# Second layer's A and B operands split ahead of the first step, in a two-layer FFN kernel on one core

## The reference, cut to what matters

```
# layer 0: mixing of channels by weights that depend on the condition, then a base product with LoRA
agg_w = einsum('bk,koi->boi', softmax(mlp(cond)), weight)    # a 32x32 matrix for each batch
c0    = einsum('boi,bih->boh', agg_w, x) + agg_b
x     = x + c0 @ W_base.T + b_base + sum over 4 experts of alpha_e * 2 * (c0 @ A_e.T) @ B_e.T
# layer 1: a grouped convolution of 9 taps along the columns, then a base product with LoRA, top 2 of 28
c1     = conv(x, weight, groups=4) + cond @ c_weight.T + bias
logits = c1 @ gate_W.T                                       # the two largest, with a softmax
x      = x + c1 @ base_W.T + (gate * 2 * (c1 @ lora_A.T)) @ lora_B.T
```

## Time and profile before

| what | value |
|---|---|
| median of 3 runs | 385.61 us (385.39 to 385.76) |
| the profiled execution, own time | 385.73 us |
| its span | 383.8 us |
| PE, DVE, ACT, POOL busy | 97%, 70%, 32%, 15% of the span |
| granted TensorE clock | 0.998 of full speed |

### The profile page before, as it was taken

The page is one execution under the profiler, slowest core; times in us unless marked ns, Lnnn a source line. Parts: engine busy times, 40 slices in busy tenths (PEclk is TensorE's granted clock), DMA queues, the critical chain, the costliest instruction groups (busy, mean ns, idle before and its releaser), DMA issues.

```text
span 383.8 us, 9759 instructions
## 1 busy us (share of the span) xinstructions
PE 373.9 (97%) x3199; PEld 328.6 (86%) x3199; DVE 270.4 (70%) x935; ACT 122.6 (32%) x380; POOL 56.9 (15%) x180
## 2 busy tenths in 40 slices
PE   8999899999999999999999999999999999998996
PEld 8899689888888988888899888889988888887684
DVE  5679887676667767766786676668767666776754
ACT  6656333323323332231233323223332322222211
POOL 5459700000000000000000000000000000010000
PEclk9999999999999999999999999999999999999999
DMA  7765677655566775555767655576765556566631
GB/s 230 257 201 141 166 192 194 186 130 154 160 170 170 186 186 132 163 155 159 185 170 192 151 147 154 154 188 164 192 170 141 151 154 154 140 172 160 160 87 55
DMA packets 71018, 63.05 MB, mean 164 GB/s; under 512 B 4030, under 2 KB 53502, under 8 KB 70872
## 3 DMA queue, kind: packets, MB, share of 16 engines
q1 hardware_dynamic: 70998, 62.82, 61.5%
q10 hardware_dynamic: 2, 0.00, 0.0%
HBM read 45.75 MB, written 16.91 MB: 163 GB/s over the span
## 4 chain that ended last, share of the span: by engine, by line
PE 85%; DVE 4%; DMA 4%; SPq 3%; issue 2%; ACT 1%; ACTq 0%; DVEq 0%
PE p_chy L980 14%; PE p_chy L986 14%; PE p_chy L981 14%; PE p_u L980 8%; PE p_u L986 8%; PE p_chy L1124 8%; PE p_u L981 8%; PE p_t L1136 3%; PE p_y L980 2%; PE p_y L981 2%; PE p_y L986 2%; DMA b_raw<-b_raw 2%; DMA win<-x_scratch 1%; PE p_y L1108 1%; PE p_y L1109 1%
## 5 line engine op out<-in xcount | busy, mean ns | idle before, releaser
L980 PE MATMUL p_u<-w_hi,xt_hi 128*128 128x256 f32 (+1 forms) x256 | 69.2, 297 | 0.7 <-DVE w_lo L727 0.3
L981 PE MATMUL p_u<-w_lo,xt_hi 128*128 128x256 f32 (+1 forms) x256 | 67.1, 288 | 0.0
L821 DVE STREAM_TRANSPOSE c<-p_chy 128x512 f32<-128x512 f32 x32 | 22.9, 716 | 54.1 <-PE p_chy L1124 54.1
L539 ACT CAST u_hi<-p_u 128x256 fp32r<-128x256 f32 x64 | 24.9, 389 | 100.3 <-PE p_u L986 100.3
L591 ACT CAST g1t_hi<-p_t 112x256 fp32r<-112x256 f32 x32 | 12.0, 374 | 121.0 <-PE p_t L1136 121.0
L980 PE MATMUL p_chy<-w_hi,c_hi 128*128 128x512 f32 x124 | 49.7, 401 | 0.3 <-DVE w_lo L747 0.3
L980 PEld LDWEIGHTS p_u<-w_hi,xt_hi 128*128 128x128 f32 x256 | 48.1, 188 | 1.6 <-issue 0.7
L981 PE MATMUL p_chy<-w_lo,c_hi 128*128 128x512 f32 x124 | 48.6, 392 | 0.0
L981 PEld LDWEIGHTS p_u<-w_lo,xt_hi 128*128 128x128 f32 x256 | 48.2, 188 | 0.0
L986 PE MATMUL p_u<-w_hi,xt_lo 128*128 128x256 f32 (+1 forms) x256 | 42.9, 290 | 0.0
L986 PEld LDWEIGHTS p_u<-w_hi,xt_lo 128*128 128x128 f32 x256 | 36.2, 189 | 0.0
(11 more groups left out here) (164 smaller groups left out, 788.0 us busy)
## 6 DMA issues: line engine op xcount, KB each, us to landing
win<-x_scratch SPq DMA_DIRECT2D x96, 256.0 KB, 4.0
x_scratch<-x SPq DMA_DIRECT2D x32, 260.0 KB, 2.1
xt_sb<-in_xt SPq DMA_DIRECT2D x32, 256.0 KB, 4.9
x_sb<-in_x SPq DMA_DIRECT2D x32, 256.0 KB, 4.8
out<-y_sb SPq DMA_DIRECT2D x32, 256.0 KB, 4.0
w_sb<-in_w SPq DMA_DIRECT2D x4, 256.0 KB, 5.3
w_sb<-in_w SPq DMA_DIRECT2D x1, 1024.0 KB, 5.3
a_sb<-in_a SPq DMA_DIRECT2D x1, 504.0 KB, 7.6
```

What stands on the lines that cost most here:

```text
L539: nc.scalar.copy(u_hi[:, t.mod(4), cols], p_u[:, banks]).then_inc(u_hi_done[half], 1)
L821: V.transpose(c1[:], p_cv).then_inc(c1_tr, 1)
L980: mm(psum, lhs_hi, rhs_hi, start=start and n == 0, stop=False)
L981: mm(psum, lhs_hi, rhs_lo, start=False, stop=False)
```

## The change

Everything named here is computed as before; the order and the engines of some one-time work differ.

- a1 is loaded by ACT's queue, behind the second gelu. b1 takes its slot in SP's queue, behind w1.
- Ahead of the first step ACT writes a_hi, copies p_mix to mix_raw (both halves) and writes b_hi before u_hi of tile 1, half b. DVE writes a_lo and, in one piece, b_lo, which POOL did in four.
- w1's split moves up: the two w_hi into steps 0 and 1, both w_lo into step 1.
- ACT's constant rows of the windows' slot 1 move to the third step, behind xt_hi; PE waits for them before the second convolution instead of the first.
- b_round and mix_hi of tile 1 on ACT move behind the first exponent of layer 0's gates, into the first step.
- POOL's late mix copies are put into a function, with the same order and place.

```diff
             sp.dma_start(w_sb[:], w1.rearrange("p (c d) -> p c d", c=HC)).then_inc(ld_w1, 16)
-            sp.dma_start(a1_sb[:], a1.rearrange("p (c n) -> p c n", c=HC)).then_inc(ld_a1, 16)
+            sp.dma_start(b1_sb[:], b1.rearrange("p (a d) -> p a d", a=2)).then_inc(ld_b1, 16)
...
-            b1_v = b1.rearrange("p (a d) -> p a d", a=2)
-            sp.dma_start(b1_sb[:], b1_v).then_inc(ld_b1, 16)
...
+            def late_mix(blocks):
+
+                for k in blocks:
+                    pool.tensor_copy(*raw_blocks(k // BT, k % BT)).then_inc(mix_rest_done, 1)
+                    pool.wait_ge(mix_rest_done, k + 1)
+
...
-                        for n in range(BT):
-                            for b in range(BT):
-                                pool.tensor_copy(*raw_blocks(n, b)).then_inc(mix_rest_done, 1)
-                                pool.wait_ge(mix_rest_done, n * BT + b + 1)
+                        late_mix(range(0, MIX_REST))
...
-                if at(s, 1):
-                    pool.wait_ge(b1_hi_done, 1)
-                    pool.wait_ge(wc_beta_done, 2)
-                    for n in range(BT):
-                        a, cols = n // 2, slice(n % 2 * NY, (n % 2 + 1) * NY)
-                        pool.tensor_tensor(b1_lo[:, a, cols], b1_sb[:, a, cols], b1_hi[:, a, cols].bitcast(f32), ALU.subtract).then_inc(b1_lo_done, 1)
-                        pool.wait_ge(b1_lo_done, n + 1)
...
+            act.dma_start(a1_sb[:], a1.rearrange("p (c n) -> p c n", c=HC)).then_inc(ld_a1, 16)
             act.wait_ge(am_max_done, 1)
...
-            act.wait_ge(ident_done, 1)
-            nc.scalar.copy(win[KIM:KC, 1].rearrange("k (b g) q -> k b (g q)", g=GROUPS),
-                           ident[KIM:KC, KIM:KC].unsqueeze(2).to_broadcast([BT, BT, GROUPS * NQ])).then_inc(batch_rows_done, 1)
+            act.wait_ge(ld_a1, 16)
+            nc.scalar.copy(a1_hi[:], a1_sb[:]).then_inc(a1_hi_done, 1)
+            act.wait_ge(mix_mm, 1)
+            raw_copied(0)
+            raw_copied(1)
             u_high(first, "b")
             act.wait_ge(mix_zeroed, 1)
-            act.wait_ge(mix_mm, 1)
             mix_copies(FIRST, range(BT // 2))
...
             xt_high(third)
+            act.wait_ge(ld_b1, 16)
+            nc.scalar.copy(b1_hi[:], b1_sb[:]).then_inc(b1_hi_done, 1)
             u_high(second, "b")
...
-            act.wait_ge(copied_b, 16 * 4)
-            nc.scalar.copy(b0_round[:], b0_raw[:]).then_inc(b0_round_done, 1)
-            mix_high(second)
...
                 if at(s, 0):
                     z0_exponent(s)
-                    raw_copied(0)
+                    act.wait_ge(rsw0_done, 1)
+                    act.wait_ge(rsw0b_done, 1)
+                    act.wait_ge(ld_rows_b, 16 * ACT0)
+                    act.wait_ge(copied_b, 16 * 4)
+                    nc.scalar.copy(b0_round[:], b0_raw[:]).then_inc(b0_round_done, 1)
+                    mix_high(s + 1)
                     u_high(s + 1, "a")
                     xt_high(s + 3)
                     u_high(s + 2, "b")
                     g0t_copied(s)
-                    raw_copied(1)
+                    w1_high(0)
...
                     u_high(s + 2, "a")
-                    act.wait_ge(ld_a1, 16)
-                    nc.scalar.copy(a1_hi[:], a1_sb[:]).then_inc(a1_hi_done, 1)
+                    w1_high(1)
                     xt_high(s + 4)
                     u_high(s + 3, "b")
-                    w1_high(0)
                     u_high(s + 3, "a")
                     g0t_copied(s)
                     mix_high(s + 2)
-                    w1_high(1)
                 elif at(s, 2):
                     u_high(s + 3, "b")
-                    act.wait_ge(ld_b1, 16)
-                    nc.scalar.copy(b1_hi[:], b1_sb[:]).then_inc(b1_hi_done, 1)
                     c1_high(s + -LAG)
                     u_high(s + 3, "a")
                     z0_exponent(s)
                     xt_high(s + 4)
+                    act.wait_ge(ident_done, 1)
+                    nc.scalar.copy(win[KIM:KC, 1].rearrange("k (b g) q -> k b (g q)", g=GROUPS),
+                                   ident[KIM:KC, KIM:KC].unsqueeze(2).to_broadcast([BT, BT, GROUPS * NQ])).then_inc(batch_rows_done, 1)
                     t_exponent(s + -LAG)
...
             xt_low(second)
+            dve.wait_ge(a1_hi_done, 1)
+            V.tensor_tensor(a1_lo[:], a1_sb[:], a1_hi[:].bitcast(f32), ALU.subtract).then_inc(a1_lo_done, 1)
             u_low(first, "b")
             dve.wait_ge(mix_zeroed, 1)
-            dve.wait_ge(mix_mm, 1)
+            dve.wait_ge(raw_act_done, 2)
...
+            dve.wait_ge(b1_hi_done, 1)
+            V.tensor_tensor(b1_lo[:], b1_sb[:], b1_hi[:].bitcast(f32), ALU.subtract).then_inc(b1_lo_done, 1)
             u_low(second, "b")
...
                     xt_low(s + 4)
-                    dve.wait_ge(a1_hi_done, 1)
-                    V.tensor_tensor(a1_lo[:], a1_sb[:], a1_hi[:].bitcast(f32), ALU.subtract).then_inc(a1_lo_done, 1)
+                    w1_low(0)
                     u_low(s + 3, "a")
-                    w1_low(0)
+                    w1_low(1)
                 elif at(s, 2):
                     u_low(s + 3, "b")
                     residual(s + -1)
                     c1_transposed(s + -LAG)
                     c1_low(s + -LAG)
-                    w1_low(1)
                     z0_logits(s)
...
                         pe.wait_ge(ld_wc, 32)
-                        pe.wait_ge(batch_rows_done, 1)
                         pe.wait_ge(batch_rows_0, 1)
                         pe.wait_ge(rsw0_done, 1)
+                    if at(v, 1):
+                        pe.wait_ge(batch_rows_done, 1)
...
                 if at(s, 2):
-                    pe.wait_ge(b1_lo_done, BT)
+                    pe.wait_ge(b1_lo_done, 1)
```

More of the change, by code:

```diff
@@ L545, in mix_copies, with raw_copied @@
                         nc.scalar.copy(*mix_blocks(tiles, n, b)).then_inc(mix_act_done, 1)
+            def raw_copied(n):
+                half = slice(n * RAW, (n + 1) * RAW)
+                nc.scalar.copy(mix_raw[:, half], p_mix[:, half]).then_inc(raw_act_done, 1)
             def w0_high(c):
@@ L580, in _ @@
             nc.scalar.copy(b0_raw[3 * L0N:3 * L0N + 3, 0:NY], p_rsw0["a"][3 * L0N:3 * L0N + 3]).then_inc(rsw0_done, 1)
-            act.wait_ge(rsw0_done, 1)
-            act.wait_ge(rsw0b_done, 1)
-            act.wait_ge(ld_rows_b, 16 * ACT0)
-            act.wait_ge(copied_b, 16 * 4)
-            nc.scalar.copy(b0_round[:], b0_raw[:]).then_inc(b0_round_done, 1)
-            mix_high(second)
             def step(s):
@@ L619, in w1_high @@
                     nc.scalar.copy(w1_hi[:, half], w_sb[:, half]).then_inc(w1_hi_done, 1)
-                def raw_copied(n):
-                    half = slice(n * RAW, (n + 1) * RAW)
-                    nc.scalar.copy(mix_raw[:, half], p_mix[:, half]).then_inc(raw_act_done, 1)
                 if at(s, 0):
                     z0_exponent(s)
-                    raw_copied(0)
+                    act.wait_ge(rsw0_done, 1)
[4 more added lines that the diff above has]
+                    mix_high(s + 1)
                     u_high(s + 1, "a")
```

## The result

The changed kernel takes 386.62 us (median of 14 runs, 385.61 to 389.51), the kernel before 385.63 (14 runs in the same rounds): ratio 1.0033, 95% interval 1.0021 to 1.0044. It is slower by 1.0 us. The forecast was 384.7 and the range ended at 385.9. Run again beside others it took 386.58 (10 runs).

The account below looks back on a forecast made before the run. PE, busy 97% of 383.8 us, was taken as the bound, with waits to win before 48 us. 385.73 - 1.9 (third step) + 1.0 (start) = 384.8, less 0.12 for the median: 384.7 us, range 383.6 to 385.9.

Parts of the forecast that it names:

- -1.9 us in the third step: Net gain on PE in the third step: 2.2 us of waits less 0.3, bounds 1.2 and 2.4.
- +1.0 at the start: Loss at the start: after b_hi and b_lo, PE gets the next u_lo 1.0 us later, including 0.6 at the first.
- The third step's 2.2 us: PE's waits to be won there: 0.47 us on w_lo, 1.49 before the transpose of g0, 0.2 on x.
- the win copy: ACT's constant win rows, 1.90 us, ahead of t_exp and g0t in the third step: 0 to 0.5 exposed, 0.3 taken.
- what is late next is x of tile 2: In the third step, x of tile 2, behind t_exp, would be the next thing late, by 0.3 us as taken.
- 1.49 us: PE's wait before the transpose of g0 in the third step, from DVE's and POOL's g0s; it would go whole.
- up to 0.3 us: Possible further gain from DVE and POOL sharing a port pair, with a_lo or w_lo beside the late mix.
- The landing: b1's load in a1's old slot behind w1 would land at 20.3 us, bounds 18.9 and 22.
- D: Early a1 delays first-layer operands: 385.7 to 386.2 us, chance 0.10; sign: PE's mix matmuls over 0.5 us late.
- The forecast's own rule: At the start, each us that b1 lands after 20.3 holds ACT, DVE and so PE for one us.
- rival C: Slower because b1 lands late at the start: a landing at 22.2 gives 386.6 us; chance 0.10.

Follow-up runs that it names:

- e16: The changed kernel run again, unchanged, beside other kernels: 386.58 us, ratio 1.0029 to the kernel before.
- e10: The kernel before with only b1 loaded behind w1 and split by ACT and DVE ahead of u of tile 1, no b_lo on POOL: 386.08 us.
- e8: The changed kernel with b1's load, ACT's b_hi and POOL's b_lo put back to their old places: 383.98 us.
- e13: e10 with a1 loaded by ACT's queue behind the second gelu: 386.69 us.
- e2: The kernel before with POOL's four b_lo pieces moved behind its g0s of tile 2: 385.62 us, ratio 1.0005.
- e11: The kernel before with PE made to wait for b1's load ahead of u of tile 2: 389.87 us.
- e14: The changed kernel with a1 issued by SP behind the third xt instead of by ACT: 388.20 us.
- e3: The changed kernel with 16 matmuls of ones, results unused, where PE waits for u_lo of tile 1: 388.72 us.
- e7: The changed kernel with 8 filling matmuls of ones ahead of u of tile 2: 389.24 us.
- e12: The kernel before with 14 matmuls of ones, results unused, on PE ahead of u of tile 2: 388.17 us.

## Why the prediction was wrong

The sum was -1.9 us in the third step and +1.0 at the start. The waits that it named at both places were real, but two of its steps failed. The start costs 1.8 to 2.4 us at u of tile 2 instead of 1.0, since b1 lands at 21.0 to 21.7 and not at 20.3. And what takes over in the third step is the load of the windows, not x of tile 2.

**The third step's 2.2 us were there, what takes over was misnamed.** Both losses that it measured are gone in the changed kernel, POOL's g0s is early, and the win copy costs 0.5 to 0.6 us (0.3 taken). But the step "what is late next is x of tile 2" failed: it is win's load of tile 1. The store (2.1 us), three issues and the load (4.8 us) follow x of tile 1. In the kernel before, the last of the three was issued at 40.8 and took 4.8 us, so the windows had landed at 45.6 for a convolution at 46.02. A PE that comes 2 us earlier without an earlier x meets them: 1.6 us in the profiled run, 1.3 over two tiles in e16. The forecast priced each wait on PE and never asked when the data of the next stages land.

**POOL's part was priced at the wrong place.** The forecast split 1.49 us into 0.5 for DVE and 1.0 for POOL's late g0s, and let DVE's chain get shorter by w_lo's 1.3 us only. The pieces of b_lo on POOL also lengthened that chain, by 1.2 us from z to ntop (3.70 to 2.51 in e10), which stands nowhere in its sum. Each half of the change wins 1.5 us between the first convolution and mixing of tile 3 (e8, e10). The forecast's comparison of a_lo's 1.59 us with w_lo's 1.30 doesn't carry its up to 0.3 us: the other w_lo, at 35.64, ran beside the late mix too and took 1.25.

**The start: a term mis-sized, with the right mechanism.** ACT waits for b_sb, DVE and u of tile 1 stand behind it, and g0s and the next u_lo behind these, in the order given. The landing was put at 20.3 and came at 21.7; the loss was put at 1.0 and was 2.4 at u of tile 2, half a, in the profiled run and 1.8 in e16 (landing 21.0; 0.7 of it was there before u of tile 1, see D below). b1 was priced by a1's landing in the same slot, as if a1's new place had no effect on it; e10 and e13 show that it has, about 1 us. The forecast's own rule, a us of time for each us of landing, gives 2.4 for 21.7. This is rival C, which had 0.10. What a late start costs up to the first convolution, another 1.2 us in e16, was not in the sum either.

**The clock was not in the sum.** A wait of 2 us on PE was priced at 2 us. In the profiled run 2.7 us more were lost at 1.2 GHz; of the 14 runs the four slowest (387.4 to 389.5) have mean clocks of 0.991 to 0.996, the others 0.997 or more.

**D was absent from the profiled run, not from the kernel.** There the mix matmuls start at 11.71 (11.99 before), and u_hi at 14.76. But in e16 they start at 12.69, 0.7 us late, which is more than the 0.5 that the forecast named as D's sign; PE waited 1.5 us for w0's low part before them. In the thirteen traces with a1 loaded early they start between 11.7 and 12.7, seven of them after 12.1; in the five with a1 loaded late, between 11.5 and 12.0. So early a1 does harm in two places, on the first layer's operands in some runs, and on b1.

## What to carry to other kernels

A wait for a load put in front of an engine's running work must be priced by that load's last share, and by every load that the same change moves ahead of it. Before counting a removed wait as won, ask for each input of the next stages when it lands now and what sets that; here windows that landed 0.4 us ahead of their use became a wait of 1.6. The longest wait named for the bound engine may lie beside a longer chain, so read the chain of waits and not only the list. Work moved from one place to a later one beside the same chain can still slow it (e2); taking it away is another experiment (e10).

## What was not expected of the hardware

- After 2.1 us of idle time on PE its clock was at 1.2 GHz for some 6.7 us (changed kernel), and in e11, with 2.4 us of idle time, for 3.4 us; after 2.0 us in e14's trace it stayed at 2.4 GHz. Matmuls that start 0.12 us apart then start 0.21 apart. In the traces with that stretch filled by matmuls (e3, e7, e12) it stayed at 1.00, but four of e7's six runs have mean clocks of 0.991 to 0.996.
- The last of the sixteen shares of the load behind the 1 MB one lands 1.5 us after the other fifteen in the kernel before and 2.2 us in the changed one, and the instruction that waits for the load starts then (b_hi at 21.69).
- Some DVE instructions of 0.2 us took 0.6 to 0.7 while POOL subtracted b_lo beside them (three of them in e2).
